# Two passes of 256 tokens for the last expert, and a new order of gating, statistics and maximum behind it

## What is computed

```python
x = x + tanh(g_xattn[0]) * differential_attention(layernorm(x), ctx)
# mixture of 8 experts, all of them computed for every token, gate = top-p of a softmax
h = relu(einsum('bth,ehf->betf', layernorm(x), W1) + b1)        # E = 8, F = 512
y = einsum('betf,efh->beth', h, W2) + b2
x = x + tanh(g_ffn[0]) * einsum('bte,beth->bth', gate, y)
x = x + tanh(g_xattn[1]) * attention(layernorm(x), ctx)         # 16 heads
# fake-quantised feed-forward: ONE scale from the largest value of the whole input
n = layernorm(x)                                                # (x - mean) / sqrt(var + 1e-5)
scale = sigmoid(clip_x) * max(abs(n)) / 127
xq = clip(round(n / scale), -128, 127) * scale
x = x + tanh(g_ffn[1]) * ffn(xq)                                # gate, up, silu, quantise again, down
```

## Times and profile before

| | us |
|---|---|
| median of 3 runs (171.52 to 173.4) | 171.95 |
| the profiled execution, its own time | 172.18 |
| span of that profile, first to last instruction | 170.4 |
| TensorE busy | 157.6 (92%) |
| Vector engine busy | 130.4 (76%) |
| Scalar engine busy | 104.3 (61%) |
| GpSimd busy | 63.0 (37%) |

### The profile page before, as it was taken

How to read it: one execution, slowest core, us unless ns; L and a number is a source line. 1 busy time by engine, 2 the same in 40 slices (tenths; PEclk the granted TensorE clock), 3 DMA queues, 4 the chain that set the end, 5 groups by cost and what they waited for, 6 DMA issues and landing times.

```text
span 170.4 us, 2664 instructions
## 1 busy us (share of the span) xinstructions
PE 157.6 (92%) x854; PEld 126.8 (74%) x854; DVE 130.4 (76%) x320; ACT 104.3 (61%) x291; POOL 63.0 (37%) x75
## 2 busy tenths in 40 slices
PE   5998889999999989999999999999999999878882
PEld 5696777768887857778878877688887989757860
DVE  2666878995784699995797879887964676879892
ACT  3367688767957657758466348999335252349161
POOL 3221678577166988242000163030070322304300
PEclk9999999999999999999999999999999999999999
DMA  5899206614776332100000611010101000000004
GB/s 146 224 327 337 97 30 240 237 47 147 168 283 229 95 153 62 37 28 0 2 2 10 187 58 51 10 61 0 67 23 38 0 0 4 2 0 0 0 4 123
DMA packets 8324, 15.04 MB, mean 88 GB/s; under 512 B 1091, under 2 KB 3299, under 8 KB 8310
## 3 DMA queue, kind: packets, MB, share of 16 engines
q1 hardware_dynamic: 7830, 14.62, 26.5%
q10 hardware_dynamic: 480, 0.25, 0.5%
HBM read 14.29 MB, written 0.57 MB: 87 GB/s over the span
## 4 chain that ended last, share of the span: by engine, by line
PE 53%; DVE 21%; ACT 8%; DMA 7%; POOL 5%; issue 3%; SPq 1%; DVEq 0%; ACTq 0%
PE ps L743 48%; PE ps L740 5%; DVE hlo L1375 4%; DMA raw<-in_experts 4%; ACT hhi L644 2%; DMA early_sb<-in_early 2%; POOL raw L375 1%; DVE xn L1180 1%; DVE stats L1170 1%; DVE xs L1234 1%; ACT raw L508 1%; DVE dif L1267 1%; POOL w2lo L384 1%; DMA gates_dram<-xT 1%; ACT ytmp L713 1%
## 5 line engine op out<-in xcount | busy, mean ns | idle before, releaser
L1375 DVE SCALAR_TENSOR_TENSOR hlo<-ps,hhi 128x512 fp32r<-128x512 f32 x64 | 43.8, 686 | 19.9 <-ACT hhi L644 19.5
L644 ACT ACTIVATE hhi<-ps 128x512 fp32r<-128x512 f32 x64 | 37.9, 598 | 31.4 <-PE ps L743 30.7
L743 PE MATMUL ps<-xhi,w1hi 128*128 128x512 f32 x64 | 30.2, 471 | 0.9 <-DVE hlo L1375 0.7
L743 PE MATMUL ps<-hlo,w2hi 128*128 128x512 f32 x64 | 25.3, 396 | 0.0
L743 PE MATMUL ps<-hhi,w2lo 128*128 128x512 f32 x64 | 25.2, 394 | 0.0
L743 PE MATMUL ps<-xhi,w1lo 128*128 128x512 f32 x64 | 25.1, 393 | 0.0
L743 PE MATMUL ps<-hhi,w2hi 128*128 128x512 f32 x64 | 25.1, 393 | 0.0
L743 PE MATMUL ps<-xlo,w1hi 128*128 128x512 f32 x64 | 25.1, 392 | 0.0
L363 POOL TENSOR_TENSOR rstd<-ve,mhalf 128x2 f32<-128x2 f32 (+1 forms) x12 | 8.9, 740 | 38.2 <-DVE ve L1175 38.2
L743 PEld LDWEIGHTS ps<-xhi,w1hi 128*128 128x128 f32 x64 | 12.1, 188 | 5.4 <-issue 2.5
L743 PEld LDWEIGHTS ps<-ident 128*128 128x128 f32 x104 | 14.4, 208 | 2.2 <-POOL ident L389 1.7
(11 more groups left out here) (192 smaller groups left out, 298.5 us busy)
## 6 DMA issues: line engine op xcount, KB each, us to landing
G<-gates_dram SPq DMA_DIRECT2D x16, 256.0 KB, 3.7
raw<-in_experts SPq DMA_DIRECT2D x7, 512.0 KB, 5.0
w1r<-in_experts SPq DMA_DIRECT2D x8, 256.0 KB, 4.1
l1w<-in_l1w SPq DMA_DIRECT2D x4, 512.0 KB, 7.6
l1w<-in_ffnw SPq DMA_DIRECT2D x1, 560.0 KB, 3.2
raw<-in_experts SPq DMA_DIRECT2D x2, 256.0 KB, 6.2
early_sb<-in_early SPq DMA_DIRECT2D x1, 333.0 KB, 3.3
xs<-in_x SPq DMA_DIRECT2D x2, 128.0 KB, 2.7
```

The source lines that it names most:

```text
L644: eng.activation(hhi[:, n % 4, :], ps[:, UPB[n % 3], :], ACT.Relu).then_inc(s["hi_ready"], 1)
L743: return eng.matmul(dst, lhsT, rhs, start=start, stop=stop)
L1375: eng.scalar_tensor_tensor(hlo[:, n % 4, :], ps[:, UPB[n % 3], :], 0.0, hhi[:, n % 4, :].bitcast(F32), ALU.max, ALU.subtract).then_inc(s[" ...
```

## The change

- `TILES` grows from 64 to 68: the last expert of the second half is done in tiles 60 to 63 for its first 256 tokens and in 64 to 67 for the other 256 (`tokens_of`). Products, high and low parts of these eight tiles have 256 columns. The second pass sums in `YB[16]`, another bank.
- `gated_last(0)` gates the first 256 tokens behind the low part of tile 66, `gated_last(1)` the others. TensorE sums and transposes tiles 4 and 5 in `last_sum(0)`, between `down(64)` and `down(65)`, and tiles 6 and 7 in `last_sum(1)` behind the last `down`.
- The first maximum stands behind the low part of tile 67; then come `residual2(0)`, `gated_last(1)`, `stats2(0)`, `residual2(1)`, `stats2(1)`.
- Epsilon is added for these four token tiles by GpSimd (`inv_std`), not by the Vector engine.

```diff
@@
         s = {n: sem(n) for n in names}
 
 
-        TILES = 2 * E * FT
+        FULL = 2 * E * FT - FT
+        TILES = FULL + 2 * FT
         LAG = 3
         UPB = [0, 1, 2]
         YB = [4, 5, 3] + [4, 5] * 7
@@
             return max((j for j in range(k) if YB[j] == YB[k]), default=-1)
 
         def tile_of(n):
+            if n >= FULL:
+                return 1, E - 1, (n - FULL) % FT
             return n // (E * FT), n // FT % E, n % FT
+        def tokens_of(n):
+            return slice(0, HT) if n < FULL else slice(0, HT // 2) if n < FULL + FT else slice(HT // 2, HT)
 
 
         PREP = ([("kT", a, n, 0, 6 + u % 2) for u, (a, n) in enumerate(G3)]
@@
                 eng.wait_ge(s["ve_ready"], n)
                 eng.tensor_tensor(rstd[:, t0:t1], ve[:, t0:t1], mhalf[:, t0:t1], ALU.pow).then_inc(s["rstd_ready"], 1)
 
+            def inv_std(n, t0, t1):
+                eng.wait_ge(s["ve_ready"], n)
+                step(eng.tensor_scalar(ve[:, t0:t1], mv[:, t0:t1, 1], 1.0, EPS, ALU.mult, ALU.add))
+                eng.tensor_tensor(rstd[:, t0:t1], ve[:, t0:t1], mhalf[:, t0:t1], ALU.pow).then_inc(s["rstd_ready"], 1)
             def inv_rms(c):
                 t0, t1 = CH_T0[c], CH_T0[c] + 2
                 eng.wait_ge(s["sq_ready"], c + 1)
@@
                 add_y(k)
             inv_root(10, 0, 2)
             add_y(2 * E - 2)
-            inv_root(11, 4, 6)
-            inv_root(12, 6, 8)
+            inv_std(11, 4, 6)
+            inv_std(12, 6, 8)
 
             eng.wait_ge(s["sxi_ready"], 1)
             eng.tensor_scalar(gsx[:], wsc[:, 0:6], sx[:], None, ALU.mult).then_inc(s["gsx_ready"], 1)
@@
                 eng.wait_ge(s["up_done"], n + 1)
                 if n >= 4:
                     eng.wait_ge(s["down_done"], n - 3)
-                eng.activation(hhi[:, n % 4, :], ps[:, UPB[n % 3], :], ACT.Relu).then_inc(s["hi_ready"], 1)
+                c = tokens_of(n)
+                eng.activation(hhi[:, n % 4, c], ps[:, UPB[n % 3], c], ACT.Relu).then_inc(s["hi_ready"], 1)
                 if n == 1:
                     router_exp(0)
                 if n in (14, 17):
@@
                 if n >= 3:
                     eng.wait_ge(s["lo_ready"], n - 2)
                 wh, wl = w1hi[:, e, ft * P:(ft + 1) * P], w1lo[:, e, ft * P:(ft + 1) * P]
-                t = slice(half * HT, (half + 1) * HT)
-                dst = ps[:, UPB[n % 3], :]
+                c = tokens_of(n)
+                t = slice(half * HT + c.start, half * HT + c.stop)
+                dst = ps[:, UPB[n % 3], c]
                 mm(dst, wh, xhi[:, t], True, False)
                 mm(dst, wh, xlo[:, t], False, False)
                 if half == 0 and ft == 0:
@@
 
             def down(n):
                 half, e, ft = tile_of(n)
-                k = half * E + e
+                k = half * E + e + (n >= FULL + FT)
+                c = tokens_of(n)
                 if ft == 0:
                     if half == 0:
                         eng.wait_ge(s["w2_split"], e + 1)
@@
                     if k == 2:
                         eng.wait_ge(s["pevac_a"], on_act(N_VOT - 1))
                 wh, wl = w2hi[:, e, ft * D:(ft + 1) * D], w2lo[:, e, ft * D:(ft + 1) * D]
-                dst = ps[:, YB[k], :]
+                dst = ps[:, YB[k], c]
                 eng.wait_ge(s["lo_ready"], n + 1)
-                mm(dst, wh, hhi[:, n % 4, :], ft == 0, False)
-                mm(dst, wh, hlo[:, n % 4, :], False, False)
-                mm(dst, wl, hhi[:, n % 4, :], False, ft == FT - 1).then_inc(s["down_done"], 1)
+                mm(dst, wh, hhi[:, n % 4, c], ft == 0, False)
+                mm(dst, wh, hlo[:, n % 4, c], False, False)
+                mm(dst, wl, hhi[:, n % 4, c], False, ft == FT - 1).then_inc(s["down_done"], 1)
+            def last_sum(part):
+                if part == 0:
+                    eng.wait_ge(s["y_done"], adds(2 * E - 2))
+                    eng.wait_ge(s["x3_ready"], B)
+                for j in range(2):
+                    t = 2 * part + j
+                    mm(ps[:, ACCB[part] + j, 0:P], acc[:, t * P:(t + 1) * P], ident[:], True, False)
+                eng.wait_ge(s["y_mul"], 2 * E + part)
+                for j in range(2):
+                    t = 2 * part + j
+                    last = mm(ps[:, ACCB[part] + j, 0:P], ytmp[:, (2 * E - 1) % 2, t * P:(t + 1) * P], ident[:], False, True)
+                last.then_inc(s["acct_ready"], 1)
 
             for n in range(TILES):
                 up(n)
@@
                     transposed_probs(1, 1)
                 if n == 59:
                     attend1(1, 0, NB)
+                if n == TILES - 1:
+                    last_sum(0)
             for n in range(TILES - LAG, TILES):
                 down(n)
-            eng.wait_ge(s["y_done"], adds(2 * E - 2))
-            eng.wait_ge(s["x3_ready"], B)
-            for t in range(HTILE):
-                mm(ps[:, ACCB[t // 2] + t % 2, 0:P], acc[:, t * P:(t + 1) * P], ident[:], True, False)
-            for t in range(HTILE):
-                if t % 2 == 0:
-                    eng.wait_ge(s["y_mul"], 2 * E + t // 2)
-                last = mm(ps[:, ACCB[t // 2] + t % 2, 0:P], ytmp[:, (2 * E - 1) % 2, t * P:(t + 1) * P], ident[:], False, True)
-                if t % 2 == 1:
-                    last.then_inc(s["acct_ready"], 1)
+            last_sum(1)
 
             def normalised_transposes(n, t0, t1):
 
@@
                     eng.wait_ge(s["acct_ready"], 1)
                 if k >= 3:
                     eng.wait_ge(s["y_done"], adds(k - 2))
-                for t in (slice(0, HT),) if k < 2 * E - 1 else (slice(0, HT // 2), slice(HT // 2, HT)):
-                    eng.scalar_tensor_tensor(acc[:, t] if e == 0 else ytmp[:, k % 2, t], ps[:, YB[k], t], b2T[:, e:e + 1],
-                                             G[:, k % 3, t], ALU.add, ALU.mult).then_inc(s["y_mul"], 1)
+                eng.scalar_tensor_tensor(acc[:] if e == 0 else ytmp[:, k % 2, :], ps[:, YB[k], :], b2T[:, e:e + 1],
+                                         G[:, k % 3, :], ALU.add, ALU.mult).then_inc(s["y_mul"], 1)
+            def gated_last(part):
+                k = 2 * E - 1
+                c = tokens_of(FULL + FT * part)
+                eng.wait_ge(s[f"g_loaded{k % 3}"], 16 * (k // 3 + 1))
+                eng.wait_ge(s["down_done"], FULL + FT * (part + 1))
+                eng.wait_ge(s["y_done"], adds(k - 2))
+                eng.scalar_tensor_tensor(ytmp[:, k % 2, c], ps[:, YB[k + part], c], b2T[:, E - 1:E], G[:, k % 3, c],
+                                         ALU.add, ALU.mult).then_inc(s["y_mul"], 1)
 
             def add_y(k):
 
@@
 
             for n in range(TILES):
                 eng.wait_ge(s["hi_ready"], n + 1)
-                eng.scalar_tensor_tensor(hlo[:, n % 4, :], ps[:, UPB[n % 3], :], 0.0, hhi[:, n % 4, :].bitcast(F32),
+                c = tokens_of(n)
+                eng.scalar_tensor_tensor(hlo[:, n % 4, c], ps[:, UPB[n % 3], c], 0.0, hhi[:, n % 4, c].bitcast(F32),
                                          ALU.max, ALU.subtract).then_inc(s["lo_ready"], 1)
                 half, e, ft = tile_of(n)
                 if n == 0:
@@
                     normalise(10, 0, 2).then_inc(s["xq_ready"], 1)
                 if n == 62:
                     gated(2 * E - 2)
+                if n == FULL + FT + LAG - 1:
+                    gated_last(0)
+            def residual2(i):
+                t0 = HTILE + 2 * i
+                eng.wait_ge(s["acct_ready"], 2 + i)
+                eng.scalar_tensor_tensor(xs[:, t0:t0 + 2, :], ps[:, ACCB[i]:ACCB[i] + 2, 0:P], gth[:, 2:3],
+                                         xs[:, t0:t0 + 2, :], ALU.mult, ALU.add).then_inc(s["xb_ready"], 1)
+            def stats2(i):
+                eng.wait_ge(s["xb_ready"], i + 1)
+                t0 = HTILE + 2 * i
+                for j in range(t0, t0 + 2):
+                    last = eng.bn_stats(stats[:, j, :], xs[:, j, :])
+                after(step(last))
+                for j in range(t0, t0 + 2):
+                    last = eng.bn_aggr(mv[:, j, :], stats[:, j, :])
+                last.then_inc(s["ve_ready"], 1)
 
             eng.wait_ge(s["xq_ready"], 1)
-            eng.tensor_reduce(xmx[:, 0:1], xn[:, 0:4, :], mybir.AxisListType.XY, ALU.max, apply_absolute_value=True).then_inc(
-                s["xmx_ready"], 1)
-            gated(2 * E - 1)
+            eng.tensor_reduce(xmx[:, 0:1], xn[:, 0:4, :], mybir.AxisListType.XY, ALU.max,
+                              apply_absolute_value=True).then_inc(s["xmx_ready"], 1)
             eng.wait_ge(s["row_added"], 3)
-            for i, t0 in enumerate((4, 6)):
-                eng.wait_ge(s["acct_ready"], 2 + i)
-                eng.scalar_tensor_tensor(xs[:, t0:t0 + 2, :], ps[:, ACCB[i]:ACCB[i] + 2, 0:P], gth[:, 2:3], xs[:, t0:t0 + 2, :], ALU.mult, ALU.add).then_inc(s["xb_ready"], 1)
-                eng.wait_ge(s["xb_ready"], i + 1)
```

(6 more changed lines are left out.)

## The result

| | median us | lowest to highest | runs |
|---|---|---|---|
| before | 171.96 | 171.14 to 222.98 | 14 |
| changed | 171.31 | 170.63 to 173.57 | 14 |

The ratio is 0.9954, 95% interval 0.9931 to 0.9976: 0.5% faster, less than 1%. Ratios are taken over the executions within 1.5% of the fastest of their kernel, so the single one of 222.98 isn't in them. The profiled execution took 171.05 with a span of 169.3.

The account below looks back on a forecast made before the run. TensorE bounds until the last down product, then the Vector engine's tail. Normalising tiles 4 and 5 at 146.15 instead of 146.54 saves 0.39: 171.8 from the profiled 172.18, 171.6 from the median 171.95. Range 170.8 to 172.9.

Parts of the forecast that it names:

- the likeliest case: Normalisation of tiles 4 and 5 starts 0.39 us sooner, giving 171.6; gain 0.2 to 0.6, chance 0.60.
- rival 4: Larger gain, 170.9 to 171.3: half matmuls spaced 0.112 and GpSimd's short epsilon price of 0.19 holds; chance 0.12.
- Half matmuls at 0.118: TensorE, last expert: 48 matmuls of 256 columns come every 0.118 us, 5.66 in all against 5.55 as 24 full ones.
- Rival 3: Weight loads bound the half matmuls at a spacing of 0.188 us: slower, 174.9; chance 0.08.
- rival 2: The gain is used up, 171.8 to 172.4: a fixed fee makes a half matmul take 0.125 us; chance 0.20.
- Last down product 1.08 later: TensorE issues the last down product until 143.21, 1.08 us later, as half the summing moves ahead of three down products.
- The tie ahead of the first `ytmp` product: In the first sum, the Vector engine's first gating ends at 141.67 and TensorE finishes `acc` at 141.71.
- Pipeline slack costs nothing: Half tiles on TensorE, Scalar and Vector engines: 1.07 us needed of 1.77 available, slack 0.7, costed at nothing.
- The Vector engine's tail 2.58: Vector engine from second gating at 143.47 through both pairs' statistics to 146.05: 2.58 us instead of 4.15.
- GpSimd's first addition at 0.52: GpSimd's epsilon addition for tiles 4 and 5 takes 0.52 us, so the Vector engine can normalise at 146.15.
- A fixed run of 1.99: TensorE from the first normalised pair's transposes to the Vector engine's read of the three maxima: unchanged at 1.99 us.
- TensorE's floor with 0.2 to spare: TensorE reaches the transposes of tiles 4 and 5 at about 146.6, normalised tiles at 146.76; limits gain to about 0.6.

Follow-up runs that it names:

- The doubled additions: Changed kernel with GpSimd's epsilon addition done twice, for tiles 4 and 5 or for 6 and 7: residual to maxima 14.21 or 14.41 us, against 14.13.
- the removed fillers: Changed kernel without three filler matmuls on TensorE, ahead of the first pair's transposes or between the pairs: residual to maxima 14.13 us both times.
- epsilon alone: Kernel before with only epsilon for tiles 4 to 7 moved to GpSimd: residual to maxima 14.30 us against 14.49, ratio to before 1.0014.

## Why the prediction was right

The time of 171.31 lies in the range, and the gain of 0.39 in the likeliest case (171.6) is within 0.03 of what the stretch shows, 0.36. The medians are 0.65 apart, though, more than the 0.2 to 0.6 of the forecast case and next to the 170.9 to 171.3 of rival 4. Of that rival's two conditions one came true (the short GpSimd price) and the other not (a spacing of 0.112). By its steps:

- **Half matmuls at 0.118:** measured 0.118. The row that decided was the one with two loads 0.12 apart, not the 0.188 of the records. Rival 3 is out, and so is rival 2 with its 0.125.
- **Last down product 1.08 later:** 1.11.
- **The tie ahead of the first `ytmp` product:** the gating was there at 140.77, TensorE ready at 140.85. No wait, with 0.08 to spare.
- **Pipeline slack costs nothing:** right, but only because of the sum between. Without it the last low part costs 0.13, which the prediction's general slack of 0.7 did not show: behind the last `up` there is less work between than in the middle of the loop.
- **The Vector engine's tail 2.58:** 2.50 (142.72 to 145.22), with an idle 0.13 ahead of `residual2(1)` where the sum had none.
- **GpSimd's first addition at 0.52: wrong.** It took 0.19 after 4.7 of idling, so the Vector engine decided, and tiles 4 and 5 were normalised 0.54 sooner, not 0.39. The 0.52 of the earlier trace rows is not the price of a first addition, and the rows were misread: the addition of 0.19 at 60.34 also stood straight behind other work, this one:

```profile
59.06 1.30 POOL L379 TENSOR_TENSOR w1lo<-raw,w1hi 128x512 fp32r<-128x512 f32 x1
```

- **"A fixed run of 1.99": wrong.** It became 2.19. I followed the chain of waits from the first pair and gave the second no sum of its own, though epsilon lengthened exactly its path on GpSimd. Already before, its power ended at 147.43 and the Vector engine came to it at 147.51 (the rows shown with the result): 0.08 to spare. The doubled additions (0.28 against 0.08) and the removed fillers (nothing) show that the second pair ends the stretch now. The two errors, 0.15 too little and 0.20 too much, cancelled: a good part of the accuracy is luck.
- **TensorE's floor with 0.2 to spare:** by the prediction's own rows (143.92 to 146.7, less 0.46) TensorE gets there at 144.40 + 2.32 = 146.72, 0.04 ahead of 146.76 and not 0.2. Its fillers did end level with the normalisation, but it was no floor (removed, nothing came).
- **Nothing ahead of tile 60 moves:** in the profiled execution it did, by 0.63 and 0.15, which the prediction had named as a sign of being wrong. Traces of the same code differ by as much, as the next paragraphs say.

Of the parts, the split alone costs 0.24, the new order behind it earns 0.60 (14.73 to 14.13), and epsilon on GpSimd nothing on top, though alone it is worth 0.19. Within the new order only the place of the first sum was tested by itself (0.08); how the rest divides between the early first gating and the halved sum stays open.

**What stays open.** At full granted clock the runs of the change have a mean of 171.07 (9 of 14) and 171.21 (7 of 12), those of before 171.74 (20 of 34) and 171.64 (19 of 29), about 0.55 apart where the stretch accounts for 0.36; the kernel before against itself differs by 0.09 (171.73, 9 of 12, and 171.64). Of the 0.15 between tile 0 and the residual, both traces of the change have it (110.77 and 110.78, against 110.92 and 110.98), nearly all of it ahead of tile 24. But the ten traces with the change's code there spread from 110.25 to 111.05, the four with the code of before from 110.57 to 110.98, and in all fourteen tile 24 to tile 60 takes 69.15 to 69.19. So the 0.15 is within what executions of the same code differ by, and it can't be put down to the change. Where the rest of the 0.55 comes from, if it is more than chance, stays open.

## What to carry to other kernels

Where two pieces of work pass through the same engines one behind the other, sum both to the end: shortening the first one's path while lengthening the second's can leave the end where it was, and the chain of waits will go on naming the engine that sits between them. When a profile leaves doubt which path binds, add a small known piece to each path and see which one passes it on whole. And price a smaller matmul by the distance of two weight loads that had nothing to wait for, not by the length of their records.

## What the runs showed of the hardware

- Split-format matmuls of 128 x 128 weights start every 0.231 at 512 columns, 0.118 at 256 and 0.112 at 128. The fp32 fillers with 64 columns have 0.112 too. Each of these has a load of its own. The floor near 0.11 is shown; that the load sets it is not.
- GpSimd took 0.19 for an addition of 128 x 2 with 4.7 idle ahead of it, 0.19 with 0.44 ahead, 0.24 with 0.19 (epsilon alone) and 0.28 with 0.15: the length varies, and long idling isn't what makes it long.
- In the trace with epsilon on the Vector engine TensorE's granted clock fell behind the stretch, and the rest took 22.34 instead of 21.26. TensorE in windows (from:to length, busy (instructions), granted clock, DMA share, GB/s):

```profile
148.26:155.00 6.74, 4.83 (x36) 1.00 0.00 0
155.00:160.00 5.00, 4.32 (x38) 1.00 0.01 3
160.00:165.00 5.00, 3.82 (x24) 0.72 0.00 0
165.00:170.60 5.60, 2.28 (x13) 0.80 0.31 94
```

The 0.72 and 0.80 are means over windows that were partly at 1.2 GHz, partly at 2.4: taken by single microseconds the granted clock is 1.00 until 162, 0.60 in the next, 0.50 (1.2 GHz) from 163 to 165, 0.70 in the next and 1.00 again from 166 to 169. TensorE was busy for 0.54 of the microsecond from 161 and for 0.28 of the next; in the change's own trace it was busy for 0.31 and 0.68 of the same two, and the clock stayed full. Eleven matmuls behind it took 2.76 (from 162.72) instead of 1.87 (from 162.32), 0.89 of the 1.08 by which the rest is longer. The 1.08 is three times what the whole change is worth, and 14 of 34 runs of the kernel before had a mean clock below full. Comparing small changes by their medians alone is hard here; a stretch cut out of the trace at two common marks repeats within 0.01.
